# A fused attention and feed-forward block on one core: every fourth clip of the exponentials moves from VectorE to GpSimd

## The chip, the core and the metric

The kernel runs on one core of one Trainium2 chip. The core has five engines that run their own instruction queues and meet only at semaphores: TensorE (matrix products; PE in the profile, its weight loads PEld), VectorE (DVE), ScalarE (ACT), GpSimd (POOL) and SyncE (SP, which here only issues DMAs). The metric is the device time of one execution in microseconds; lower is better.

## The reference, cut to what matters

32 sequences of 100 rows of width 256 attend to a context of 1444 rows each, with 16 heads of width 16, and then go through a quantized feed-forward layer with 704 hidden units:

```
q, k, v = proj(layernorm(x), Wq), proj(ctx, Wk), proj(ctx, Wv)
scores = clip(q @ k.T / 4, -50, 50);  masked positions = -50
probs  = softmax(scores)
x = x + tanh(g0) * layernorm(rs * ((probs @ v) @ Wo.T + bo)) * gamma + beta
h = silu(bitlinear(layernorm(x), w1)) * bitlinear(layernorm(x), w2)
x = x + tanh(g1) * bitlinear(h, w3)
```

The clip of the scores to -50..50 is done after the exponential: the kernel bounds exp(score) from below by exp(-50) and from above by a value per context row, which is exp(50) for a valid row and exp(-50) for a masked one. All in fp32.

## The kernel before

One batch is one of the 32 sequences. Its 1444 context rows are cut into NT = 12 tiles of 121 rows (the last has 113). For every tile TensorE computes the transposed scores of all 16 heads in two halves (line 1327, tile sc), ScalarE exponentiates each half into e_sb (line 619, 121x800 elements), one instruction clips the whole tile in place (line 860, 121x1600), and TensorE multiplies it with v (line 1347, tile pvb). There are six e_sb buffers. The products with v come in blocks of VISIT = 4 tiles, after the scores of slots 1, 5 and 9.

Each engine has a function batch() that loops over twelve slots n = 0 to 11, one for each tile. The order within a slot is written out by hand, and every engine works strictly in that order. Into the slots of batch b the program also puts: the keys and values of batch b+1 (TensorE lines 1368 and 1382; ScalarE k_hi and v_sb; VectorE c_hi, c_lo and k_lo, since fp32 products are made of high and low parts), the layer norm of x of batch b+3 (tiles x_ve, x_rstd, xn), the queries of b+1 (bd, bd_hi, bd_lo, stacked into q_st by twelve DMAs that GpSimd issues), and the output of finished batches: the attention read of pvb, the quotient oT, the product with wo (line 1425), the residual and layer norms, and the feed-forward layer (hq is its quantized hidden row). The 3200 output rows are handled in 25 groups of 128, so 25 of the 32 batches complete a group (full_group).

What GpSimd does in a batch, in this order: in slot 3 it copies the upper bounds of the next batch (mask_of, hi_b) and takes an inverse square root (delta_rstd, d_r), in slot 4 another (x1_rstd), in slot 5 two small factors (ffn_factors), in slot 8 it issues the twelve q_st DMAs (stack_q), and in slot 11 it adds beta to the residual (residual, x_res) and takes the inverse square root for x of batch b+3 (x_rstd_of, x_rstd). VectorE reads that x_rstd in its own slot 11:

```
if nxt2 and b.row + 3 < NB and n == 11:
    x_norm(b.plus(3))          # waits for pool_x, writes xn
...
if n:
    clip(b, n - 1)
```

In VectorE's slot 1 stand the attention read and the inverse of the sums, in slots 1 and 2 the two k_lo of the last third of the context, in slot 2 attention_out (oT) and c_lo of the next batch.

Of the kernel before, what the change touches and what calls it, by code (L numbers as in the profile page):

```python
# [41 lines left out]
def flamingo_block(nc, x, ctxT, maskT, g_xattn, g_ffn, wqT, bq, wkT, bk, wvT, bv, woT, bo,  # L42
# [20 lines left out]
    ALU, ACT, AX = mybir.AluOpType, mybir.ActivationFunctionType, mybir.AxisListType  # L63
# [13 lines left out]
    NT = -(-T // P)  # L77
    TT = -(-T // NT)
    TL = [min(TT, T - n * TT) for n in range(NT)]
# [4 lines left out]
    STEPS = 2  # L84
# [5 lines left out]
    VISIT = 4  # L90
# [10 lines left out]
    E_LO, E_HI = float(np.exp(-CLIP)), float(np.exp(CLIP))  # L101
# [7 lines left out]
    with es:  # L109
# [6 lines left out]
        def sem(name):  # L116
            return es.enter_context(nc.semaphore(name))
# [46 lines left out]
        hi_b = [sb(f"hi_b{i}", [TT, NT]) for i in range(2)]  # L164
# [49 lines left out]
        care_c, care_k, care_v = sem("care_c"), sem("care_k"), sem("care_v")  # L214
        care_x, care_q, care_d, care_y = sem("care_x"), sem("care_q"), sem("care_d"), sem("care_y")
        sc_ready, exp_done = sem("sc_ready"), sem("exp_done")
        clip_done, pv_done = sem("clip_done"), sem("pv_done")
        pe_ctx, pe_x, pe_q, pe_post = sem("pe_ctx"), sem("pe_x"), sem("pe_q"), sem("pe_post")
        split_done, k_lo_done = sem("split_done"), sem("k_lo_done")
        k_hi_done, v_done, act_post = sem("k_hi_done"), sem("v_done"), sem("act_post")  # L220
# [1 line left out]
        act_x, act_q, result_done = sem("act_x"), sem("act_q"), sem("result_done")  # L222
        pool_x, pool_mask, pool_post = sem("pool_x"), sem("pool_mask"), sem("pool_post")

        CLEAN = ("gt", "lt", "pos", "nan", "put_gt", "put_lt")
        SPLIT = Steps(*(f"{p}{u}" for u in range(NCH) for p in ("hi", "lo")))
        CTX = Steps(*(f"{w}{u}{i}" for u in range(NCH) for w in ("k", "v") for i in range(2)))
# [34 lines left out]
        def e_slot(b, n):  # L262
            return (NT * b.par + n) % NE

        def stacked_count(b, u):
            own = b.base or isinstance(b.n, int) and b.n == NB - 1
            return 16 * 3 * NQ * (b.n + 1) - (16 * 3 * (NQ - NQ // 2) if own and u == NCH - 1 else 0)

        def asked(b):

# [169 lines left out]
        def _(pool):  # L440
# [20 lines left out]
            def mask_of(b):  # L461
                pool.wait_ge(s_setv, SETV["hi_all"])
                if b.n >= 2:
                    pool.wait_ge(clip_done, TILE.after(b.plus(-2), NT - 1))
                nc.gpsimd.tensor_copy(hi_b[b.par][:, :],
                                      hi_all[:, :, bass.ds(b.row, 1)].rearrange("p n o -> p (n o)")
                                      ).then_inc(pool_mask, 1)

            def x_rstd_of(b):
                pool.wait_ge(dve_x, X_V.after(b, "var"))  # L470
# [52 lines left out]
            def batch(b, nxt, nxt2=True):  # L523
                gd = full_group(b.plus(-1))
                for n in range(NT):
                    if n == 3:
                        if nxt:
                            mask_of(b.plus(1))
                        if gd:
                            delta_rstd(gd)  # L530
                        if not nxt and not b.base:
                            stack_last(b)
                    if n == 4 and gd:
                        x1_rstd(gd)
                    if n == 5 and gd:
                        ffn_factors(gd)
                    if n == 8 and nxt:
                        stack_q(b.plus(1))
                    if n == 11 and full_group(b):
                        residual(full_group(b))  # L540
                    if n == 11 and nxt2 and b.row + 3 < NB:
                        x_rstd_of(b.plus(3))
# [212 lines left out]
        def _(dve):  # L755
# [97 lines left out]
                                       accum_out=watched(b, KT * u + o)).then_inc(k_lo_done, 1)  # L853

            def clip(b, n):
                dve.wait_ge(exp_done, SCORE.after(b, STEPS * (n + 1) - 1))
                if n == 0:
                    dve.wait_ge(pool_mask, b.n + 1)
                e = e_sb[e_slot(b, n)][0:TL[n], :]
                V.tensor_scalar(e, e, E_LO, hi_b[b.par][0:TL[n], n:n + 1], ALU.max, ALU.min).then_inc(clip_done, 1)  # L860
# [432 lines left out]
        def _(pe):  # L1293
# [37 lines left out]

            def pv(b, n, half, first_batch=False):
                if half == 0:
                    pe.wait_ge(clip_done, TILE.after(b, n))
                    if n % 2 == 0:
                        pe.wait_ge(v_done, VE.after(b, f"{n // TPC}{(n % TPC) // 2}"))
                        if b.base:
                            pe.wait_ge(care_v, GUARD_V.after_row(b, f"{n + 1}1less"))
                    if n == 0 and not first_batch:
                        pe.wait_ge(dve_att, A_V.after(b.plus(-1), "z1"))  # L1340
                e = e_sb[e_slot(b, n)]
                for a in range(2):
                    for j in range(NQ):
                        pr = half * NQ + j
                        col = half * PW + a * S

                        last = T_.matmul(pvb[QR * j:QR * (j + 1), col:col + S],  # L1347
                                         v_sb[0:TL[n], n, pr, a:a + 2, :].rearrange("p x d -> p (x d)"),
                                         e[0:TL[n], pr * PW + a * S:pr * PW + (a + 1) * S],
                                         start=(n == 0 and half == 0 and a == 0), stop=(n == NT - 1),  # L1350
                                         skip_group_check=True)
                if half == 1:
                    last.then_inc(pv_done, 1)
# [267 lines left out]
```

## Time and profile before

| | |
|---|---|
| time, median of 3 runs | 1319.75 us (1317.11 to 1321.18) |
| the profiled execution | 1317.0 us, of which the span of the instructions 1315.2 us |
| TensorE busy | 1292.3 us, 98% of the span |
| VectorE busy | 1080.8 us, 82% |
| ScalarE busy | 951.1 us, 72% |
| GpSimd busy | 361.1 us, 27% |
| clips | 384, 403.0 us of VectorE's time |

The table's busy times are unions over the whole span. An engine that is busy for less than the span had nothing that it was allowed to do in the rest; what it waited for stands in the views of waits and of single instructions.

### The profile page before, as it was taken

Reading aid. Unit: us, or ns where it says so; the run is one execution under the profiler, and the core shown is the slowest. Engines: PE = TensorE matmul, PEld = TensorE weight load, DVE = VectorE, ACT = ScalarE, POOL = GpSimd, SP = SyncE. Lnnn points to the kernel's source line nnn. Section 1 sums busy time; section 2 is a strip of 40 time slices with the busy share of each in tenths; the row PEclk is TensorE's granted clock in tenths of the full one; section 3 lists DMA queues with packets and bytes.
Section 4 is the critical chain, followed back from the end, with each engine's and each line's share of the span. In section 5 each row is a group of like instructions: output and inputs, shape, how many; then the busy total and the mean of one; then the engine's idle time right before and its main releaser. Section 6 shows DMA issues by size and latency. Waiting matters only on the chain.

```text
span 1315.2 us, 47323 instructions
## 1 busy us (share of the span) xinstructions
PE 1292.3 (98%) x19836; PEld 1184.1 (90%) x19836; DVE 1080.8 (82%) x2167; ACT 951.1 (72%) x1576; POOL 361.1 (27%) x594
## 2 busy tenths in 40 slices
PE   8999999999999999999999999999999999999995
PEld 7999999999999989999899999999999999998985
DVE  5789888789888789886889886889778889778875
ACT  3877777867677767776867777777777767777761
POOL 3222223231233231222331222331133331122320
PEclk9999999999999999999999999999999999999989
DMA  7977667766767776777766768776777766767630
GB/s 206 254 175 169 172 164 192 192 168 166 180 155 195 189 170 164 172 166 197 183 170 166 177 159 207 174 170 164 177 186 179 178 170 163 181 174 181 150 87 12
DMA packets 121421, 225.39 MB, mean 171 GB/s; under 512 B 29675, under 2 KB 89871, under 8 KB 121199
## 3 DMA queue, kind: packets, MB, share of 16 engines
q1 hardware_dynamic: 106968, 200.58, 62.3%
q0 software_dynamic: 12576, 20.42, 6.6%
q8 instruction: 159, 2.61, 0.9%
q10 hardware_dynamic: 1654, 1.27, 0.4%
q14 instruction: 64, 0.52, 0.1%
HBM read 57.27 MB, written 3.28 MB: 46 GB/s over the span
## 4 chain that ended last, share of the span: by engine, by line
PE 79%; DVE 13%; issue 3%; POOL 2%; SPq 1%; DMA 1%; ACT 1%; ACTq 1%; DVEq 0%; POOLq 0%
PE sc L1327 19%; PE pvb L1347 18%; PE cb L1382 17%; PE cb L1368 16%; PE mb L1447 2%; DVE e_sb L860 2%; PE mb L1415 2%; DVE c_lo L827 1%; DVE k_lo L851 1%; DVE zt L945 1%; SPq L342 1%; PE mb L1425 1%; PE mb L1462 1%; DMA k_st<-k_lo 1%; PE cb L1531 1%
## 5 line engine op out<-in xcount | busy, mean ns | idle before, releaser
L619 ACT ACTIVATE e_sb<-sc 121x800 f32<-121x800 f32 (+1 forms) x768 | 645.4, 845 | 167.7 <-PE sc L1327 156.1
L1327 PE MATMUL sc<-q_st,k_st 96*121 96x200 f32 (+1 forms) x3072 | 468.1, 275 | 2.9 <-ACT e_sb L619 1.4
L1327 PEld LDWEIGHTS sc<-q_st,k_st 96*121 96x121 f32 (+1 forms) x3072 | 411.1, 185 | 32.3 <-issue 7.8
L860 DVE TENSOR_SCALAR e_sb<-e_sb,hi_b 121x1600 f32<-121x1600 f32 (+1 forms) x384 | 403.0, 1054 | 18.7 <-ACT e_sb L619 18.7
L1347 PEld LDWEIGHTS pvb<-e_sb,v_sb 121*32 121x32 f32 x12288 | 264.5, 110 | 30.6 <-issue 26.4
L1347 PE MATMUL pvb<-e_sb,v_sb 121*32 121x100 f32 x12288 | 286.2, 250 | 1.2 <-DVE e_sb L860 1.2
L851 DVE SCALAR_TENSOR_TENSOR k_lo<-cb,bk_c,k_hi 128x484 fp32r<-128x484 f32 (+1 forms) x192 | 134.6, 701 | 125.5 <-ACT k_hi L631 124.9
L1382 PE MATMUL cb<-wv_hi,c_hi 128*121 128x256 f32 (+1 forms) x768 | 223.1, 290 | 2.4 <-DVE k_lo L851 1.2
L505 POOL DMA_DIRECT2D q_st<-bd_hi x256 | 152.3, 598 | 259.0 <-DVE bd_lo L913 252.9
L1382 PE MATMUL cb<-wv_hi,c_lo 128*121 128x256 f32 (+1 forms) x768 | 216.0, 281 | 0.0
L1382 PE MATMUL cb<-wv_lo,c_hi 128*121 128x256 f32 (+1 forms) x768 | 215.7, 281 | 0.0
L1368 PE MATMUL cb<-c_hi,wk_hi 128*128 128x484 f32 (+1 forms) x384 | 153.2, 399 | 1.4 <-ACT v_sb L640 1.4
L1382 PEld LDWEIGHTS cb<-wv_hi,c_hi 128*121 128x121 f32 (+1 forms) x768 | 141.5, 184 | 6.5 <-DVE k_lo L851 6.3
L1368 PE MATMUL cb<-c_hi,wk_lo 128*128 128x484 f32 (+1 forms) x384 | 145.9, 380 | 0.0
L1368 PE MATMUL cb<-c_lo,wk_hi 128*128 128x484 f32 (+1 forms) x384 | 145.5, 379 | 0.0
L1382 PEld LDWEIGHTS cb<-wv_hi,c_lo 128*121 128x121 f32 (+1 forms) x768 | 140.8, 183 | 0.1
L1382 PEld LDWEIGHTS cb<-wv_lo,c_hi 128*121 128x121 f32 (+1 forms) x768 | 140.2, 183 | 0.0
L631 ACT ACTIVATE k_hi<-cb,bk_c 128x484 fp32r<-128x484 f32 (+1 forms) x192 | 127.0, 661 | 2.0 <-PE cb L1368 1.9
L484 POOL TENSOR_TENSOR d_r<-d_ve,minus_half 128x1 f32<-128x1 f32 x25 | 32.2, 1288 | 344.4 <-DVE d_ve L975 344.4
L827 DVE TENSOR_TENSOR c_lo<-c_in,c_hi 128x968 fp32r<-128x968 f32 (+1 forms) x96 | 117.1, 1220 | 0.0
L640 ACT ACTIVATE v_sb<-cb 121x512 f32<-121x512 f32 x160 | 96.2, 602 | 10.1 <-PE cb L1382 10.1
L1368 PEld LDWEIGHTS cb<-c_hi,wk_lo 128*128 128x128 f32 x384 | 72.1, 188 | 11.7
(165 smaller groups left out, 1358.6 us busy)
## 6 DMA issues: line engine op xcount, KB each, us to landing
k_st<-k_hi SPq DMA_DIRECT2D x508, 121.0 KB, 2.5
c_in<-in_ctxT SPq DMA_DIRECT2D x64, 484.0 KB, 3.9
k_st<-k_lo SPq DMA_DIRECT2D x254, 121.0 KB, 2.5
k_st<-k_hi SPq DMA_DIRECT2D x252, 119.0 KB, 3.2
c_in<-in_ctxT SPq DMA_DIRECT2D x32, 476.0 KB, 3.9
k_st<-k_lo SPq DMA_DIRECT2D x126, 119.0 KB, 3.0
q_st<-bd_hi POOLq DMA_DIRECT2D x256, 50.0 KB, 3.4
q_st<-bd_lo POOLq DMA_DIRECT2D x128, 50.0 KB, 3.5
```

The costliest lines, as they stand in the source:

```text
L484: nc.gpsimd.tensor_tensor(d_r[:, :], d_ve[:, :], minus_half[:, :], ALU.pow).then_inc(pool_post, 1)
L505: nc.gpsimd.dma_start(q_st[b.par][QR * part:QR * (part + 1), j, :, :].bitcast(f32), src[QR * j:QR * (j + 1), :, :, :].rearrange("p k a s - ...
L619: nc.scalar.activation(e_sb[e_slot(b, n)][0:TL[n], k * SW:(k + 1) * SW].rearrange("p (o c) -> p o c", o=2), sc[q % NSC][0:TL[n], :, 0:2 * PW],
L631: nc.scalar.activation(k_hi[slot][:, o, 0:CL[u]], cb[o][:, 0:CL[u]], ACT.Identity, bias=bk_c[:, o:o + 1]).then_inc(k_hi_done, 1)
L640: nc.scalar.activation(v_sb[0:TL[n], n:n + 2, :, 0:3:2, :].rearrange("p n q a d -> p (n q) a d"), cb[i][0:TL[n], :].rearrange("p (q a d) - ...
L827: V.tensor_tensor(c_lo[slot][:, :, 0:w], c_in[slot][:, :, 0:w], c_hi[slot][:, :, 0:w].bitcast(f32), ALU.subtract).then_inc(split_done, 1)
L851: V.scalar_tensor_tensor(k_lo[slot][:, o, 0:w], cb[o][:, 0:w], bk_c[:, o:o + 1], k_hi[slot][:, o, 0:w].bitcast(f32), ALU.add, ALU.subtract ...
L860: V.tensor_scalar(e, e, E_LO, hi_b[b.par][0:TL[n], n:n + 1], ALU.max, ALU.min).then_inc(clip_done, 1)
L1327: last = T_.matmul(sc[q % NSC][0:TL[n], e // 2, (e % 2) * PW:(e % 2 + 1) * PW], k_st[st_slot(b, n // TPC)][:, pr % NQ, pr // NQ, t0:t0 + T ...
L1347: last = T_.matmul(pvb[QR * j:QR * (j + 1), col:col + S], v_sb[0:TL[n], n, pr, a:a + 2, :].rearrange("p x d -> p (x d)"), e[0:TL[n], pr * ...
L1368: last = T_.matmul(cb[o][:, 0:w], wt[:, k, o * P:(o + 1) * P], ct[slot][:, k, 0:w], start=i == 0, stop=i == 5)
L1382: last = T_.matmul(cb[i][0:TL[n], half * H:(half + 1) * H], ct[slot][:, k, t0:t0 + TL[n]], wt[:, k, :], start=(k == 0 and a == 0), stop=(k ...
```

## The change

The clips of tiles 2, 6 and 10 of each batch are issued by GpSimd and signal a semaphore of their own, pool_clip; VectorE clips the other nine. The counts that other engines wait for are adapted, and TensorE waits for pool_clip where the tile is GpSimd's. The instruction is the same (a maximum with a constant, then a minimum with hi_b per partition, in place).

```diff
+        def by_pool(n):
+            return n % VISIT == 2
+
+        def clipped(b, n):
+            return (NT - POOL_CLIPS) * b.n + n + 1 - (n + VISIT - 2) // VISIT
...
+            def clip(b, n):
+                pool.wait_ge(exp_done, SCORE.after(b, STEPS * (n + 1) - 1))
+                e = e_sb[e_slot(b, n)][0:TL[n], :]
+                alone()
+                nc.gpsimd.tensor_scalar(e, e, E_LO, hi_b[b.par][0:TL[n], n:n + 1], ALU.max, ALU.min).then_inc(pool_clip, 1)
...
             def batch(b, nxt, nxt2=True):
                 gd = full_group(b.plus(-1))
                 for n in range(NT):
+                    if n and by_pool(n - 1):
+                        pool.wait_ge(pool_mask, b.n + 1)
+                        clip(b, n - 1)
                     if n == 3:
...
             def clip(b, n):
+                if by_pool(n):
+                    return
                 dve.wait_ge(exp_done, SCORE.after(b, STEPS * (n + 1) - 1))
...
                 if half == 0:
-                    pe.wait_ge(clip_done, TILE.after(b, n))
+                    if by_pool(n):
+                        pe.wait_ge(pool_clip, POOL_CLIPS * b.n + n // VISIT + 1)
+                    else:
+                        pe.wait_ge(clip_done, clipped(b, n))
```

GpSimd's queue around a batch boundary before the change, from the last q_st DMA of one batch (slot 8) over slot 11 to slot 5 of the next:

```order
L505 DMA q_st<-bd_hi 32x400
L478 TENSOR_TENSOR x_res<-x_res,beta_t 128x256
L471 TENSOR_TENSOR x_rstd<-x_ve,minus_half 100x1
L465 COPY hi_b<-hi_all 121x12
L484 TENSOR_TENSOR d_r<-d_ve,minus_half 128x1
L488 TENSOR_TENSOR d_rstd<-d_ve,minus_half 128x1
L493 TENSOR_TENSOR tiny<-tiny,k_tanh 128x1
L496 TENSOR_SCALAR tiny<-tiny,wmean 128x1
L505 DMA q_st<-bd_hi 32x400
```

The same stretch of GpSimd's queue in the changed kernel, whose lines are numbered a little higher:

```order
L520 DMA q_st<-bd_hi 32x400
L482 TENSOR_SCALAR e_sb<-e_sb,hi_b 121x1600
L493 TENSOR_TENSOR x_res<-x_res,beta_t 128x256
L486 TENSOR_TENSOR x_rstd<-x_ve,minus_half 100x1
L482 TENSOR_SCALAR e_sb<-e_sb,hi_b 121x1600
L473 COPY hi_b<-hi_all 121x12
L499 TENSOR_TENSOR d_r<-d_ve,minus_half 128x1
L503 TENSOR_TENSOR d_rstd<-d_ve,minus_half 128x1
L508 TENSOR_TENSOR tiny<-tiny,k_tanh 128x1
L511 TENSOR_SCALAR tiny<-tiny,wmean 128x1
L482 TENSOR_SCALAR e_sb<-e_sb,hi_b 121x1600
L520 DMA q_st<-bd_hi 32x400
```

The clip of tile 10 now stands ahead of x_res and x_rstd, that of tile 2 ahead of hi_b, and that of tile 6 ahead of the DMAs.

VectorE's queue before the change, from slot 10 of a batch to slot 0 of the next (gs, th, tiny and hq belong to the feed-forward layer):

```order
L851 SCALAR_TENSOR_TENSOR k_lo,watch<-cb,bk_c,k_hi 128x484
L1022 SCALAR_TENSOR_TENSOR th<-th,gs 128x352
L860 TENSOR_SCALAR e_sb<-e_sb,hi_b 121x1600
L1028 TENSOR_TENSOR gs<-th,us 128x352
L887 TENSOR_SCALAR xn<-x_in,mv,x_rstd 100x256
L860 TENSOR_SCALAR e_sb<-e_sb,hi_b 121x1600
L1032 TENSOR_REDUCE tiny<-gs 128x1
L860 TENSOR_SCALAR e_sb<-e_sb,hi_b 113x1600
```

The same slots of VectorE's queue in the changed kernel:

```order
L869 SCALAR_TENSOR_TENSOR k_lo,watch<-cb,bk_c,k_hi 128x484
L1042 SCALAR_TENSOR_TENSOR th<-th,gs 128x352
L880 TENSOR_SCALAR e_sb<-e_sb,hi_b 121x1600
L1048 TENSOR_TENSOR gs<-th,us 128x352
L907 TENSOR_SCALAR xn<-x_in,mv,x_rstd 100x256
L1052 TENSOR_REDUCE tiny<-gs 128x1
L880 TENSOR_SCALAR e_sb<-e_sb,hi_b 113x1600
```

The clip of tile 10, between xn and the maximum of the hidden layer, is gone; xn stands where it stood.

## Rows read from the trace of the kernel before

**Rows 1.** Page: the span, and busy time and share of each engine.

```profile
span 1315.2 us, 47323 instructions
...
PE 1292.3 (98%) x19836; PEld 1184.1 (90%) x19836; DVE 1080.8 (82%) x2167; ACT 951.1 (72%) x1576; POOL 361.1 (27%) x594
```

**Rows 2.** Windows: length, busy time of each engine, clock, DMA share, GB/s.

```profile
600.00:1240.00 640.00, 638.40 (x9990) 586.18 (x9992) 538.31 (x1076) 477.60 (x788) 186.01 (x299) 1.00 0.72 175
```

**Rows 3.** Waits between 120 and 1240 us: total us, times, longest.

```profile
DVE k_lo L851 <- ACT k_hi L631: 109.0, 77, 3.9
...
PEld cb L1382 <- DVE k_lo L851: 4.7, 17, 0.4
PEld pvb L1347 <- DVE e_sb L860: 2.0, 6, 0.3
```

**Rows 4.** Groups by form: the full-size clips; busy us, mean ns, idle before.

```profile
L860 DVE TENSOR_SCALAR e_sb<-e_sb,hi_b 121x1600 f32<-121x1600 f32 x352 | 369.6, 1055 | 11.8 <-ACT e_sb L619 11.8
```

**Rows 5.** Groups by form: GpSimd's own instructions.

```profile
L496 POOL TENSOR_SCALAR tiny<-tiny,wmean 128x1 f32<-128x1 f32 x25 | 11.9, 477 | 5.4 <-POOL tiny L493 5.4
...
L493 POOL TENSOR_TENSOR tiny<-tiny,k_tanh 128x1 f32<-128x1 f32 x25 | 4.7, 190 | 78.8 <-DVE tiny L1007 78.8
...
L452 POOL MEMSET v_sb<- 121x1536 f32 x1 | 1.4, 1367 | 0.0
...
L450 POOL TENSOR_SCALAR_AFFINE_SELECT identf<-identf 128x128 f32<-128x128 f32 x1 | 0.3, 284 | 0.3 <-POOL minus_half L447 0.3
...
L447 POOL MEMSET minus_half<- 128x1 f32 x1 | 0.1, 113 | 0.0
```

**Rows 6.** Timeline of GpSimd, 606 to 708 us: start, duration, instruction, idle before.

```profile
608.93 0.50 POOL L505 DMA_DIRECT2D q_st<-bd_lo  x1
...
609.93 0.75 POOL L478 TENSOR_TENSOR x_res<-x_res,beta_t 128x256 f32<-128x256 f32 x1
610.88 0.56 POOL L471 TENSOR_TENSOR x_rstd<-x_ve,minus_half 100x1 f32<-100x1 f32 x1 [0.20 <-DVE x_ve L881]
...
688.47 1.53 POOL L478 TENSOR_TENSOR x_res<-x_res,beta_t 128x256 f32<-128x256 f32 x1
690.34 0.79 POOL L471 TENSOR_TENSOR x_rstd<-x_ve,minus_half 100x1 f32<-100x1 f32 x1 [0.35 <-DVE x_ve L881]
```

**Rows 7.** Timeline of VectorE, 686 to 708 us, slot 11 to slot 2.

```profile
694.07 0.41 DVE L887 TENSOR_SCALAR xn<-x_in,mv,x_rstd 100x256 f32<-100x256 f32 x1
694.39 1.04 DVE L860 TENSOR_SCALAR e_sb<-e_sb,hi_b 121x1600 f32<-121x1600 f32 x1
...
701.43 0.42 DVE L934 TENSOR_SCALAR pT<-pvb,submask 128x200 f32<-128x200 f32 x1 [0.51 <-PE pvb L1347]
...
704.77 0.61 DVE L851 SCALAR_TENSOR_TENSOR k_lo<-cb,bk_c,k_hi 128x476 fp32r<-128x476 f32 x1
...
705.31 0.36 DVE L951 TENSOR_TENSOR oT<-pT,zt 128x200 f32<-128x200 f32 x1
...
706.94 1.16 DVE L827 TENSOR_TENSOR c_lo<-c_in,c_hi 128x968 fp32r<-128x968 f32 x1
```

**Rows 8.** Timeline of ScalarE: second halves of tile 10 and tile 2.

```profile
692.58 0.88 ACT L619 ACTIVATE e_sb<-sc 121x800 f32<-121x800 f32 x1
...
705.18 0.84 ACT L619 ACTIVATE e_sb<-sc 121x800 f32<-121x800 f32 x1 [0.53 <-PE sc L1327]
```

**Rows 9.** Timeline of TensorE, 705 to 710 us.

```profile
706.12 0.29 PE L1382 MATMUL cb<-wv_hi,c_hi 128*121 128x256 f32 x1
...
706.84 1.03 PE L1425 MATMUL mb<-wo,oT 128*128 128x256 f32 x4
...
709.24 0.40 PE L1368 MATMUL cb<-c_hi,wk_hi 128*128 128x484 f32 x1
```

**Rows 10.** Timelines of VectorE around 608 and 688 us: c_lo.

```profile
608.28 1.67 DVE L827 TENSOR_TENSOR c_lo<-c_in,c_hi 128x952 fp32r<-128x952 f32 x1
...
688.27 1.14 DVE L827 TENSOR_TENSOR c_lo<-c_in,c_hi 128x952 fp32r<-128x952 f32 x1
```

More of the change, by code:

```diff
@@ L216, in flamingo_block @@
         sc_ready, exp_done = sem("sc_ready"), sem("exp_done")
-        clip_done, pv_done = sem("clip_done"), sem("pv_done")
+        clip_done, pool_clip, pv_done = sem("clip_done"), sem("pool_clip"), sem("pv_done")
         pe_ctx, pe_x, pe_q, pe_post = sem("pe_ctx"), sem("pe_x"), sem("pe_q"), sem("pe_post")
@@ L223, in flamingo_block @@
         pool_x, pool_mask, pool_post = sem("pool_x"), sem("pool_mask"), sem("pool_post")
+        POOL_CLIPS = 3
         CLEAN = ("gt", "lt", "pos", "nan", "put_gt", "put_lt")
@@ L463, in mask_of @@
                 if b.n >= 2:
-                    pool.wait_ge(clip_done, TILE.after(b.plus(-2), NT - 1))
+                    pool.wait_ge(clip_done, clipped(b.plus(-2), NT - 1))
                 nc.gpsimd.tensor_copy(hi_b[b.par][:, :],
```

## The prediction

> **What bounds the kernel now.** I read the header and the busy line of the page first, then the engines' busy time in a long stretch, then the waits, and last the timelines of one batch boundary. The span is 1315.2 us, and TensorE is busy for 1292.3 us of it [rows 1]. Between 600 and 1240 us it is busy for 638.4 of 640 us at a granted clock of 1.00 [rows 2]: in the steady part of the kernel TensorE never stands still. What it waits for there is tiny: between 120 and 1240 us its weight loads waited 4.7 us for k_lo and 2.0 us for clipped tiles [rows 3]. VectorE is busy for 82% of the span [rows 1] and has holes, above all while it waits for ScalarE's k_hi, 109.0 us in the same stretch [rows 3]. So VectorE is not the bound, but it feeds the bound. A faster VectorE can give back at most what TensorE waits for, and every microsecond by which something TensorE needs comes too late is a microsecond of the kernel's time.
>
> **What is taken away.** Three of twelve clips in each of 32 batches leave VectorE: 96 instructions of 1.055 us [rows 4], 101 us of its 1080.8. Since TensorE waited some 7 us for VectorE in the steady part, this is worth 0 to 7 us by itself. I take 0: the gain is used up as soon as one of the waits below appears.
>
> **What is added: the length of a GpSimd clip.** No 1600-column computation of GpSimd is in this trace, so I bound its duration D from other rows [rows 5]. A two-operation TENSOR_SCALAR with an operand per partition takes 0.477 us on one column: that is the fixed part. The slope is between two rows. A memset writes 1536 columns in 1.367 us and one column in 0.113, 0.82 ns a column: D = 0.48 + 1.31 = 1.8 us. An addition with two inputs takes 0.75 us on 256 columns at its fastest [rows 6] against 0.19 us for a product on one column [rows 5], 2.2 ns a column: D = 0.48 + 3.5 = 4.0 us. The nearest row is the affine select, one input read and something computed on each element: 0.284 us for 128 columns, less 0.113, is 1.33 ns a column: D = 2.6 us. I take 2.4, a little below, since a part of the select's time is a fixed one that the memset doesn't have. Either way the clip is about twice as long as on VectorE.
>
> The Trainium skill (GPSIMD Engine Reference, section 4.1) calls one-input work on GpSimd roughly line-rate. By that the columns would take 1.3 us at the 1.2 GHz which the same page states, an estimate that lies below my lower bound, and the sum below would shrink to a few microseconds.
>
> **First wait: the queue behind the clip of tile 10.** TensorE needs tiles 2, 6 and 10 only in its PV blocks, more than 5 us after they are exponentiated, so the clips themselves are in time. What stands behind them in GpSimd's queue is not. In slot 11 GpSimd used to run the residual and x_rstd as soon as the q_st DMAs were issued: x_rstd ended at 690.34 + 0.79 = 691.1 [rows 6], and VectorE read it in xn at 694.07 [rows 7]. Now both stand behind the clip of tile 10, which waits for ScalarE's exponential, finished at 692.58 + 0.88 = 693.46 [rows 8]. Add D, 0.75 for the residual and 0.56 for x_rstd [rows 6]: xn can start at 694.8 + D, that is D + 0.7 late. If VectorE's own work must first let GpSimd in (next part), up to 0.7 more. Behind xn on VectorE's queue stand the clip of tile 11, the hidden layer's quantization, the last two k_lo, the attention read and oT. The lag shrinks by the clip of tile 10 that is gone (1.04 at 694.39) and by the 0.51 that VectorE used to stand idle before the attention read at 701.43 [rows 7]. What is left at the k_lo of 704.77 is D - 0.8 to D - 0.1. That k_lo ended at 704.77 + 0.61 = 705.38 [rows 7], and TensorE used it at 706.12 [rows 9]: slack 0.74. So TensorE stands still for D - 1.5 to D - 0.8, with D = 2.4 for 0.9 to 1.6 us.
>
> **Second wait: two engines at one SBUF port.** The trace shows that VectorE and GpSimd hold each other up. The same c_lo subtraction takes 1.14 us at 688.27 and 1.67 us at 608.28 [rows 10], and in the second case GpSimd's DMA issue of 0.50 us begins at 608.93 [rows 6], while c_lo is under way. The other way round, the residual takes 0.75 us alone and 1.53 us when it starts at 688.47 [rows 6], 0.2 us into the c_lo of 688.27: it ends only after c_lo has. So whoever is second waits until the first is done. The Trainium skill (SBUF — State Buffer, section "Who interferes with whom") says just this of fp32 tensor_scalar and of instructions with two SBUF inputs on VectorE against any GpSimd instruction that reads; the trace agrees. By that rule a clip on GpSimd takes a stretch of D away from VectorE's clips, c_lo and oT where before a clip of 1.05 us stood, and in the sum it is the difference between the two values that follow.
>
> The exponential of tile 2 ends at 705.18 + 0.84 = 706.02 [rows 8], and the idle GpSimd starts at once. VectorE's oT, which had started at 705.31 [rows 7], is by then late by the lag above, so it finds the port taken, ends at 706.02 + D + 0.36, and TensorE's product with wo, due at 706.84 [rows 9], starts D - 0.4 late. That is counted from TensorE's old times, so it contains the first wait instead of adding to it: 2.0 us for D = 2.4. The c_lo behind it (706.94 to 708.10, needed at 709.24 [rows 7, 9]) is then no later than TensorE itself.
>
> **The sum.** Both steps need a batch with a full row group (residual and wo product now) after one with a hidden layer under way. Of the 29 boundaries with an xn three batches ahead, 25 groups in 32 batches leave 15 such. 15 x 2.0 = 30 us. In the other 14 the residual or the hidden layer's work is missing and the first wait is mostly absorbed, but the clip of tile 2 still meets clip 1 and c_lo: from nothing to D less c_lo's slack of 1.14, 1.3 us; I take the middle, 0.65, so 9 us. Setup and tail: 0. Together 39 us. The profiled execution had 1317.0 us of time around a span of 1315.2, so it would read 1356; against the median of 1319.75, **1359 us**, +3.0%.
>
> Other moves cost nothing. The clip of tile 6 delays the twelve q_st DMAs behind it by up to D, but GpSimd then waits for tile 10's exponential anyway, and TensorE asks for q_st only in the next batch; the residual used to start at 688.47 behind the last of them [rows 6], 5 us before that exponential [rows 8]. Were this cover gone, TensorE would wait up to D for q_st in each batch. delta_rstd, behind the clip of tile 2, is wanted by VectorE only after the wo product, which waits longer. SP's queue is untouched.
>
> **The rivals.**
> - A slower clip: D from 3 to 4 us. Then 15 x 3.6 and 14 x 2.9 at the upper end, +95: 1375 to 1415. For it speaks that residual and rstd on this engine are slow for their size.
> - Small loss: D = 1.8, GpSimd gets in at once, oT isn't blocked. 15 x 0.3 = 5 us, up to 15 with something from the rest: 1324 to 1335. The line-rate rule of the Trainium skill (GPSIMD Engine Reference, section 4.1) would lead here or below.
> - No change, 1320: D below 1.5 and no block. Only the slack of 0.74 at k_lo and that of the wo product have to hold [rows 7, 9].
> - Faster: VectorE's 101 us of relief are what TensorE's 7 us of waits come from, and nothing new is late. It takes D under 1.3, so that xn is on time within the clip saved, and gives 1312 to 1315. Against it: the memset row alone puts D at 1.8.
>
> **How the numbers follow.** Two measurements of this kernel can be told apart from about 0.3%, 4 us. Forecast (1335 to 1375): 0.60. Slower clip: 0.15. Small loss: 0.12. No change: 0.08. Faster: 0.05. Slower altogether 0.87. The range that leaves no more than 0.2 out is 1326 to 1400; it takes in most of both neighbours of the forecast.
>
> **What the changed profile would show.** GpSimd's clip at 2.4 us (1.8 to 4.0) x96. VectorE's clips x288. A wait of xn for x_rstd, 2 to 4 us in most batches, some 80 us in all, where now it is nothing. TensorE waiting for k_lo and oT, 1 to 2 us a time, its busy share in the steady part down from 99.8% to about 97%; c_lo or oT with durations above 2 us where they meet a GpSimd clip. The prediction is wrong if xn doesn't wait, if D is under 1.5, or if VectorE's late work is absorbed before TensorE asks for it; then the time stays near 1320. If TensorE waits for the GpSimd clips themselves, or for q_st, it is worse than I say.

## The result and the profile after

The changed kernel takes **1656.22 us** (median of 4 runs, 1650.04 to 1665.12) against 1318.43 us for the kernel before in the same comparison (4 runs, 1315.49 to 1321.18): ratio 1.2565, 95% interval 1.2527 to 1.2603. That is 338 us slower. The forecast was 1359 us: the direction was right, the size far off, and the time lies outside the range.

The header and busy line of the page of the changed kernel, which answer to [rows 1]:

```profile
span 1663.3 us, 47418 instructions
...
PE 1421.0 (85%) x19836; PEld 1279.9 (77%) x19836; DVE 1245.5 (75%) x2071; ACT 966.0 (58%) x1576; POOL 942.3 (57%) x690
```

The span grew by 348.1 us (the profiled run was the slowest of the four, 1665.12 us). TensorE stands still for 1663.3 - 1421.0 = 242.3 us instead of 22.9, so 219 us are new waits. The other 129 us are busy time: the same 19836 products take 1421.0 us instead of 1292.3. VectorE has 96 instructions less and is busy for 165 us more.

Two windows of the changed kernel (length, busy time of PE, PEld, DVE, ACT and POOL, granted clock, DMA share, GB/s), the first of which answers to [rows 2]:

```profile
600.00:1240.00 640.00, 552.12 (x7800) 497.45 (x7801) 477.64 (x805) 382.07 (x623) 372.97 (x270) 0.92 0.56 139
850.00:860.00 10.00, 8.20 (x36) 7.40 (x37) 8.72 (x17) 3.98 (x8) 5.56 (x4) 0.66 0.44 119
```

The granted clock of the steady part fell from 1.00 to 0.92; in the ten microseconds behind a long wait it averages 0.66, so TensorE ran there for a good part at 1.2 GHz instead of 2.4.

The groups of instructions of the changed kernel. The number behind the second bar is the idle time of the engine just before them, and what ended it:

```profile
L482 POOL TENSOR_SCALAR e_sb<-e_sb,hi_b 121x1600 f32<-121x1600 f32 x96 | 568.2, 5919 | 479.6 <-issue 473.9
...
L880 DVE TENSOR_SCALAR e_sb<-e_sb,hi_b 121x1600 f32<-121x1600 f32 (+1 forms) x288 | 490.5, 1703 | 53.2 <-ACT e_sb L637 53.1
...
L907 DVE TENSOR_SCALAR xn<-x_in,mv,x_rstd 100x256 f32<-100x256 f32 x32 | 18.6, 581 | 193.8 <-POOL x_rstd L486 193.8
```

A clip on GpSimd takes 5.92 us on average, 5.65 at its shortest, where I had put 2.4. VectorE's 288 clips take 1703 ns on average instead of some 1055 [rows 4]. xn waits 193.8 us for x_rstd; before it never did.

TensorE's waits in the changed kernel (total us, times, longest):

```profile
PE cb L1391 <- DVE c_lo L845: 56.3, 13, 5.3
PE sc L1347 <- issue: 47.6, 29, 5.0
PE mb L1448 <- DVE y_out L1074: 36.8, 13, 3.4
PE pvb L1370 <- DVE e_sb L880: 24.2, 21, 2.0
PE cb L1405 <- DVE k_lo L869: 23.6, 21, 1.8
PE mb L1448 <- DVE oT L971: 15.5, 5, 3.3
```

With 12.0 us for hq they make 216 us, nearly all of the 219. The second row is TensorE's first scores of a batch, which wait for q_st (the runs below show it).

One batch boundary shows the mechanism. GpSimd, 846 to 890 us in the changed kernel (start, duration, instruction, idle before), answering to [rows 6]:

```profile
846.78 5.65 POOL L482 TENSOR_SCALAR e_sb<-e_sb,hi_b 121x1600 f32<-121x1600 f32 x1 [8.63 <-issue]
...
868.55 6.07 POOL L482 TENSOR_SCALAR e_sb<-e_sb,hi_b 121x1600 f32<-121x1600 f32 x1 [3.73 <-issue]
874.58 0.99 POOL L520 DMA_DIRECT2D q_st<-bd_hi  x1
...
881.09 0.50 POOL L520 DMA_DIRECT2D q_st<-bd_hi  x1
882.16 6.19 POOL L482 TENSOR_SCALAR e_sb<-e_sb,hi_b 121x1600 f32<-121x1600 f32 x1 [0.58 <-issue]
888.33 0.73 POOL L493 TENSOR_TENSOR x_res<-x_res,beta_t 128x256 f32<-128x256 f32 x1
889.03 0.56 POOL L486 TENSOR_TENSOR x_rstd<-x_ve,minus_half 100x1 f32<-100x1 f32 x1
```

VectorE in the same stretch of the same kernel, answering to [rows 7]:

```profile
847.88 3.38 DVE L971 TENSOR_TENSOR oT<-pT,zt 128x72 f32<-128x72 f32 x2
851.18 0.47 DVE L1074 SCALAR_TENSOR_TENSOR y_out<-mb,tiny,x 128x256 f32<-128x256 f32 x1
851.58 1.70 DVE L880 TENSOR_SCALAR e_sb<-e_sb,hi_b 121x1600 f32<-121x1600 f32 x1
...
870.82 4.65 DVE L880 TENSOR_SCALAR e_sb<-e_sb,hi_b 121x1600 f32<-121x1600 f32 x1 [1.64 <-ACT e_sb L637]
...
889.62 0.42 DVE L907 TENSOR_SCALAR xn<-x_in,mv,x_rstd 100x256 f32<-100x256 f32 x1 [6.72 <-POOL x_rstd L486]
```

And TensorE, answering to [rows 9]:

```profile
851.80 2.05 PE L1448 MATMUL mb<-wo,oT 128*128 128x256 f32 x4 [2.82 <-DVE y_out L1074]
...
856.50 0.66 PE L1391 MATMUL cb<-c_hi,wk_hi 128*128 128x484 f32 x1
...
884.92 0.64 PE L1347 MATMUL sc<-q_st,k_st 96*121 96x200 f32 x4 [1.18 <-issue]
```

Read in order: GpSimd begins the clip of tile 2 at 846.78. oT (here two instructions in one row) starts 1.1 us later and takes 3.38 us instead of 0.36; it ends at 851.26, which is 1.17 us before GpSimd's clip does. The clip behind it ends at 853.28, 0.85 us after GpSimd's clip (852.43). The clip that VectorE starts at 870.82, while GpSimd clips tile 6, takes 4.65 us and ends at 875.47, again 0.85 us after GpSimd's 874.62. After the clip of tile 10 comes xn, for which VectorE stood idle for 6.72 us. TensorE waits 2.82 us for the product with wo, and then the product takes 2.05 us instead of the 1.03 of [rows 9]: half the clock, right behind the wait. The q_st DMAs end at 881.6, and TensorE waits for them at 884.92.

### The profile page after: what moved, and what is told of

The parts are those of the page before. It is cut to its first block and busy times, and to the rows that moved or that the text cites. A ratio compares the mean times of both kernels' runs of the same rounds, so it can differ in the third digit from the quotient of the medians.

```text
span 1663.3 us, 47418 instructions
## 1 busy us (share of the span) xinstructions
PE 1421.0 (85%) x19836; PEld 1279.9 (77%) x19836; DVE 1245.5 (75%) x2071; ACT 966.0 (58%) x1576; POOL 942.3 (57%) x690
## 5 line engine op out<-in xcount | busy, mean ns | idle before, releaser
L482 POOL TENSOR_SCALAR e_sb<-e_sb,hi_b 121x1600 f32<-121x1600 f32 x96 | 568.2, 5919 | 479.6 <-issue 473.9
L1347 PE MATMUL sc<-q_st,k_st 96*121 96x200 f32 (+1 forms) x3072 | 509.7, 292 | 48.9 <-issue 47.6
L880 DVE TENSOR_SCALAR e_sb<-e_sb,hi_b 121x1600 f32<-121x1600 f32 (+1 forms) x288 | 490.5, 1703 | 53.2 <-ACT e_sb L637 53.1
L1347 PEld LDWEIGHTS sc<-q_st,k_st 96*121 96x121 f32 (+1 forms) x3072 | 451.3, 201 | 88.8 <-issue 60.6
L1391 PE MATMUL cb<-c_hi,wk_hi 128*128 128x484 f32 (+1 forms) x384 | 173.7, 452 | 58.9 <-DVE c_lo L845 56.3
L907 DVE TENSOR_SCALAR xn<-x_in,mv,x_rstd 100x256 f32<-100x256 f32 x32 | 18.6, 581 | 193.8 <-POOL x_rstd L486 193.8
L1391 PE MATMUL cb<-c_lo,wk_hi 128*128 128x484 f32 (+1 forms) x384 | 160.9, 419 | 0.0
L1391 PE MATMUL cb<-c_hi,wk_lo 128*128 128x484 f32 (+1 forms) x384 | 159.7, 416 | 0.0
L1391 PEld LDWEIGHTS cb<-c_hi,wk_hi 128*128 128x128 f32 x384 | 84.2, 219 | 61.5 <-DVE c_lo L845 58.5
L845 DVE TENSOR_TENSOR c_lo<-c_in,c_hi 128x968 fp32r<-128x968 f32 (+1 forms) x96 | 110.4, 1150 | 0.0
```

Of the source, the lines that this page charges most:

```text
L482: nc.gpsimd.tensor_scalar(e, e, E_LO, hi_b[b.par][0:TL[n], n:n + 1], ALU.max, ALU.min).then_inc(pool_clip, 1)
L845: V.tensor_tensor(c_lo[slot][:, :, 0:w], c_in[slot][:, :, 0:w], c_hi[slot][:, :, 0:w].bitcast(f32), ALU.subtract).then_inc(split_done, 1)
L907: norm = V.tensor_scalar(xn[:, :], x_in[b.par][:, :], mv[:, 0:1], x_rstd[:, :], ALU.subtract, ALU.mult)
L1347: last = T_.matmul(sc[q % NSC][0:TL[n], e // 2, (e % 2) * PW:(e % 2 + 1) * PW], k_st[st_slot(b, n // TPC)][:, pr % NQ, pr // NQ, t0:t0 + T ...
L1391: last = T_.matmul(cb[o][:, 0:w], wt[:, k, o * P:(o + 1) * P], ct[slot][:, k, 0:w], start=i == 0, stop=i == 5)
```

## The experiments

Twelve kernels ran. Each was compared with the kernel before on the same chip (1320.1 us for forms, part560, order11 and queue0; 1319.88 for tile2, tile6, tile10 and mult; 1319.12 for queue5, tile10_order, filled and pieces).

### forms: what the operation costs on a GpSimd that does nothing else

The kernel before, with seven instructions of GpSimd on a scratch tile behind all its work:

```diff
+            form(G.tensor_scalar, t, t, E_LO, hi, ALU.max, ALU.min)
+            form(G.tensor_scalar, t[:, 0:400], t[:, 0:400], E_LO, hi, ALU.max, ALU.min)
+            form(G.tensor_scalar, t, t, E_LO, E_HI, ALU.max, ALU.min)
+            form(G.tensor_scalar, t, t, E_LO, None, ALU.max)
+            form(G.tensor_scalar, t, t, hi, None, ALU.min)
+            form(G.tensor_scalar, t, t, 1.0, 0.0, ALU.mult, ALU.add)
+            form(G.tensor_copy, t[:, 0:400], t[:, 400:800])
```

> The kernel before, with seven instructions added behind GpSimd's last one, on a private tile of 121 partitions, each waiting for the one before. It measures the disputed duration by itself, nearly without VectorE beside it. Theory A, the clip costs a fixed 0.5 us and 3.4 to 3.5 ns a column whatever VectorE does: the same clip on 800 columns takes 3.2 us and on 400 columns 1.9 us. Theory B, most of the 5.9 us is waiting for VectorE's instructions: 800 columns take about 1.4 us, as a memset's 0.82 ns a column would give. If the cost is one per operation, a single maximum or minimum on 800 columns takes about half of the double one; if it is a cost of reading and writing an element, single and double ones take the same.

The timeline of GpSimd at the end of that kernel, one row for each instruction in the order of the diff:

```profile
1301.42 2.96 POOL L571 TENSOR_SCALAR tst<-tst,hi_b 121x800 f32<-121x800 f32 x1
1304.58 1.61 POOL L571 TENSOR_SCALAR tst<-tst,hi_b 121x400 f32<-121x400 f32 x1 [0.20 <-POOL tst L571]
1306.39 2.98 POOL L571 TENSOR_SCALAR tst<-tst 121x800 f32<-121x800 f32 x1 [0.20 <-POOL tst L571]
1309.56 2.22 POOL L571 TENSOR_SCALAR tst<-tst 121x800 f32<-121x800 f32 x1 [0.19 <-POOL tst L571]
1311.99 2.28 POOL L571 TENSOR_SCALAR tst<-tst,hi_b 121x800 f32<-121x800 f32 x1 [0.22 <-POOL tst L571]
1314.46 0.86 POOL L571 TENSOR_SCALAR tst<-tst 121x800 f32<-121x800 f32 x1 [0.19 <-POOL tst L571]
1315.49 0.51 POOL L571 COPY tst<-tst 121x400 f32<-121x400 f32 x1 [0.17 <-POOL tst L571]
```

800 columns in 2.96 us and 400 in 1.61 make (2.96 - 1.61) / 400 = 3.4 ns a column and 0.26 us fixed, so 1600 columns take 5.66: just the shortest clip of the changed kernel, 5.65. The operand per partition is innocent (2.98 with a constant). The cost is in the maximum and the minimum: one of them takes 2.2 us for 800 columns, a product and a sum together 0.86. VectorE ran some short instructions beside the first four and none beside the last three; one maximum (2.22) and one minimum (2.28) take the same with and without them. So GpSimd by itself is that slow.

### part560: a clip as short as the one I had assumed

The whole change, but GpSimd clips 560 columns of its tiles and VectorE the other 1040:

```diff
-                nc.gpsimd.tensor_scalar(e, e, E_LO, hi_b[b.par][0:TL[n], n:n + 1], ALU.max, ALU.min).then_inc(pool_clip, 1)
+                nc.gpsimd.tensor_scalar(e[:, 0:560], e[:, 0:560], E_LO, hi_b[b.par][0:TL[n], n:n + 1], ALU.max, ALU.min).then_inc(pool_clip, 1)
...
-                e = e_sb[e_slot(b, n)][0:TL[n], :]
+                e = e_sb[e_slot(b, n)][0:TL[n], 560 if by_pool(n) else 0:EW]
```

> The changed kernel, but GpSimd clips only columns 0 to 559 of tiles 2, 6 and 10 and VectorE columns 560 to 1599, so that GpSimd's clip takes about the 2.4 us that the forecast assumed (0.5 + 560 x 3.45 ns = 2.4). Theory A, only the duration was wrong and the sum was right for its own D: 39 us over before, 1357 us. Theory B, the cost goes in proportion to D (338 us for 5.9 us): 137 us over before, 1455 us. Theory C, the slacks were underrated and the loss begins only with a longer clip: below 1330 us.

1364.84 us, ratio 1.0339 (1.0314 to 1.0364), +45 us. GpSimd's clip:

```profile
L482 POOL TENSOR_SCALAR e_sb<-e_sb,hi_b 121x560 f32<-121x560 f32 x96 | 241.3, 2514 | 517.6 <-issue 491.4 <-ACT e_sb L637 26.2
```

With D = 2.51 my sum gives 15 x 2.11 + 14 x 0.69 = 41 us; 45 were measured. xn waits 93 us in all (I had said some 80), and the clock stays at 0.995. Near the length that I assumed, the total holds, in part by luck. Of the 47.5 us by which the span is longer, 36 are waits of TensorE and 12 are busy time. The waits are for k_lo (27.8 us), hq (7.8) and c_lo (3.7). There is none for oT or y_out, on which 15 x 2.11 rests. One boundary of this kernel, GpSimd's clip, oT and TensorE's product behind k_lo:

```profile
731.85 2.16 POOL L482 TENSOR_SCALAR e_sb<-e_sb,hi_b 121x560 f32<-121x560 f32 x1 [9.30 <-issue]
732.95 0.36 DVE L969 TENSOR_TENSOR oT<-pT,zt 128x200 f32<-128x200 f32 x1
733.09 0.38 PE L1403 MATMUL cb<-wv_hi,c_hi 128*121 128x256 f32 x1 [1.19 <-DVE k_lo L869]
```

oT runs beside the clip at its old length. The first wait of the prediction is there, as large as it said (1.19 us, within D - 1.5 to D - 0.8), and the second is not.

### order11: the queue's wait taken away

The whole change, with the residual and x_rstd ahead of the clip of tile 10:

```diff
-                    if n and by_pool(n - 1):
+                    if n and by_pool(n - 1) and n < 11:
...
                         x_rstd_of(b.plus(3))
+                    if n == 11 and by_pool(n - 1):
+                        pool.wait_ge(pool_mask, b.n + 1)
+                        clip(b, n - 1)
```

> The changed kernel with one thing moved: in slot 11 GpSimd runs the residual and x_rstd ahead of the clip of tile 10 instead of behind it. All three clips stay on GpSimd at their full length. Theory A, most of the loss is the queue behind the clip of tile 10 (xn waited 193.8 us): those waits vanish and the time falls by 150 to 200 us, to 1450 to 1500 us. Theory B, most of it is the port, VectorE held for the length of each GpSimd clip, and the wait of xn only hides what would show elsewhere: the time falls by less than 60 us, to above 1595 us.

1647.15 us, ratio 1.2473 (1.244 to 1.2506): 9 us of the 338 come back. xn's wait for x_rstd fell from 193.8 to 16.7 us, but nothing was won. GpSimd's three instructions in one slot 11 of this kernel:

```profile
864.82 0.86 POOL L493 TENSOR_TENSOR x_res<-x_res,beta_t 128x256 f32<-128x256 f32 x1
865.65 0.56 POOL L486 TENSOR_TENSOR x_rstd<-x_ve,minus_half 100x1 f32<-100x1 f32 x1
866.22 5.67 POOL L482 TENSOR_SCALAR e_sb<-e_sb,hi_b 121x1600 f32<-121x1600 f32 x1
```

And VectorE in the same slot:

```profile
865.01 7.73 DVE L883 TENSOR_SCALAR e_sb<-e_sb,hi_b 121x1600 f32<-121x1600 f32 x1
873.09 0.40 DVE L910 TENSOR_SCALAR xn<-x_in,mv,x_rstd 100x256 f32<-100x256 f32 x1
```

x_rstd is ready at 866.21, and VectorE still comes to xn only at 873.09: its own clip stands at the port for 7.73 us. It had started at 865.01, before x_rstd (865.65) and before GpSimd's clip (866.22), and both went ahead of it. In other batches xn itself stands there, whose mean rose from 581 to 2756 ns. The port takes the place of the queue in VectorE's order; the waits of TensorE stay (for y_out 47.2 us, k_lo 32.9, c_lo 32.8, q_st 48.1).

### queue0 and queue5: the queue's wait alone, with no clip on GpSimd

Both are the kernel before with one more wait of GpSimd in slot 11, ahead of the residual and x_rstd; all clips stay on VectorE. queue0 waits for the exponential of tile 10 and gives the wait without D:

```diff
+                    if n == 11:
+                        pool.wait_ge(exp_done, SCORE.after(b, STEPS * n - 1))
                     if n == 11 and full_group(b):
```

> The kernel before, all clips on VectorE, with one wait added: GpSimd's residual and x_rstd of slot 11 wait for the exponential of tile 10, as they do in the changed kernel, but no clip stands between. xn is then about 0.7 us late. By the forecast's slacks (0.51 idle and 0.74 at k_lo, with no clip taken from VectorE) this is just absorbed: 1318 us, within 0.3%. If it costs more than 5 us, the slacks at this place were overrated.

1325.42 us, ratio 1.0043 (1.0022 to 1.0064): 5.3 us, just over the 5 that I had set: the wait alone, with a clip of no length at that place, would already cost a little. queue5 waits for the next batch's first exponentials instead, about as long as the clip lasts:

```diff
+                    if n == 11 and nxt:
+                        pool.wait_ge(exp_done, SCORE.after(b.plus(1), 1))
```

> The kernel before with all twelve clips on VectorE and no clip on GpSimd, but the residual and x_rstd of slot 11 wait for the first tile's exponential of the next batch, which comes about 4 us after that of tile 10. xn is then 4.8 us late, with no port held. Theory A, the queue wait costs by itself what the slacks say: 4.8 less 0.51 and 0.74, 3.6 us in 15 boundaries and some of it in the others, 1375 to 1400 us. Theory B, without the port VectorE catches up: below 1335 us.

1423.92 us, ratio 1.0795 (1.077 to 1.082), +105 us. xn waits 149.4 us; TensorE's waits are many and short (k_lo 37.0 us in 39, the longest 1.2; e_sb 32.2 us in 45, the longest 1.2), and the clock stays at 0.993. The queue alone does such damage without a clip at the port. It is more than either end of what I had expected: my lag left TensorE's PV blocks out, where tile 11's clip, behind xn, is asked for early (19.8 of the 32.2 us are in front of the products of tile 11).

### tile2, tile6 and tile10: one clip on GpSimd at a time

```diff
-            return n % VISIT == 2
+            return n in POOL_TILES
```

POOL_TILES holds 2, 6 or 10 alone, and the counts of the semaphores follow.

> GpSimd clips tile 2 alone, VectorE the other eleven. x_rstd is not behind a clip, so the queue wait is out. Theory A, the port: GpSimd starts at the exponential of tile 2, VectorE's clip 1, c_lo or oT is held for up to 5.7 us, and c_lo has 1.14 us of slack: about 4.6 us in most of 31 batches, 1430 to 1530 us with what the clock adds. Theory B, the queue is what counts: within 1% of before.

> GpSimd clips tile 6 alone. In the changed kernel TensorE stood idle for 47.7 us in front of the first scores of a batch, which need q_st, and the q_st DMAs stand behind the clip of tile 6. Theory A, that wait is this clip's: some 1 to 2 us in most batches, 1335 to 1375 us, with the wait at the same place. Theory B, the wait comes from the whole schedule being late: within 1% of before.

> GpSimd clips tile 10 alone, with the residual and x_rstd behind it. By the forecast's sum for D = 5.9 the first wait is D + 0.7 less 1.04, 0.51 and 0.74, so 4.3 us in 15 boundaries and less in the others: 65 to 110 us over before, 1385 to 1430 us, plus what the clock adds, with waits of xn of about 6.5 us. If the three single runs add up to the 338 us of the whole change, the losses are independent; if they add up to clearly more, one hides behind the other.

| clip on GpSimd | us | ratio (95%) | more than before | clock | TensorE waits most for |
|---|---|---|---|---|---|
| tile 2 | 1437.29 | 1.0901 (1.0853 to 1.0948) | 117 | 0.963 | k_lo 36.5, c_lo 18.1, oT 13.3 |
| tile 6 | 1415.42 | 1.0712 (1.0675 to 1.075) | 96 | 0.970 | q_st 61.1 |
| tile 10 | 1452.04 | 1.0997 (1.0955 to 1.1039) | 132 | 0.965 | e_sb 56.8, k_lo 15.8, hq 11.9 |

117 + 96 + 132 = 345, against 338 for all three: each clip has its own wait, and they add. So do the parts: TensorE stands still for 74, 64 and 85 us more than before, together 223 (219 in the changed kernel), and is busy for 43, 40 and 51 us more, together 134 (129). tile2 is in the range of its theory A; tile10 is 22 us above its range, which left the clock out, with waits of xn of 6.5 us as expected. The clip of tile 6, which the prediction put at nothing and my expectation for this run at less than was measured, costs 96 us. Its rows for TensorE's scores and VectorE's clips in tile6:

```profile
L1348 PE MATMUL sc<-q_st,k_st 96*121 96x200 f32 (+1 forms) x3072 | 483.0, 281 | 63.4 <-issue 61.1 <-ACT e_sb L638 1.4 <-DMA k_st<-k_lo 0.7
...
L881 DVE TENSOR_SCALAR e_sb<-e_sb,hi_b 121x1600 f32<-121x1600 f32 x320 | 451.7, 1414 | 31.0 <-ACT e_sb L638 31.0
```

The first scores of a batch wait 30 times, 2.0 us a time; in tile10, where that clip is VectorE's, the same group has 2.9 us of idle time in all and none of it at issue. So it is the q_st DMAs behind the clip of tile 6. In tile2 the port works the other way round as well. GpSimd:

```profile
730.30 7.40 POOL L483 TENSOR_SCALAR e_sb<-e_sb,hi_b 121x1600 f32<-121x1600 f32 x1 [15.10 <-issue]
```

VectorE at the same time:

```profile
730.13 1.04 DVE L881 TENSOR_SCALAR e_sb<-e_sb,hi_b 121x1600 f32<-121x1600 f32 x1
731.09 1.16 DVE L846 TENSOR_TENSOR c_lo<-c_in,c_hi 128x968 fp32r<-128x968 f32 x1
```

VectorE's clip and its c_lo run at their old durations until 732.25, and GpSimd's clip ends at 737.70, which is 5.45 us after that: it got hardly any work done until both were through, although c_lo was started 0.79 us after it. Its mean in that kernel is 6.9 us.

### mult: the same places, a quicker operation

GpSimd multiplies by 1 and adds 0; the clip of tiles 2, 6 and 10 is left out of the computation.

```diff
-                nc.gpsimd.tensor_scalar(e, e, E_LO, hi_b[b.par][0:TL[n], n:n + 1], ALU.max, ALU.min).then_inc(pool_clip, 1)
+                nc.gpsimd.tensor_scalar(e, e, 1.0, 0.0, ALU.mult, ALU.add).then_inc(pool_clip, 1)
```

> The changed kernel with GpSimd's instruction on tiles 2, 6 and 10 replaced by a product with 1 and a sum with 0, so the clip of these tiles is left out. The form took 0.86 us on 800 columns where the clip took 2.96, so about 1.6 us on 1600: the duration that the rival with the small loss assumed. Theory A, the sum follows D: 5 to 20 us over before, 1324 to 1340 us. Theory B, a second user at the port costs by itself, whatever its duration: above 1360 us.

1358.69 us, ratio 1.0288 (1.0253 to 1.0323), +39 us, with an instruction of 1.74 us on average and a clock of 0.994. That is more than the 1340 that I had allowed. My sum with D = 1.74 gives 15 x 1.34 + 14 x 0.3 = 24 us, and the rival called small loss gave 5 to 15: both are too low at the short end. TensorE stands still for 31 us more than before and is busy for 10 us more, which is no term of the sum. Here the product with wo does wait for y_out and oT (17.6 us), and the boundaries without one wait for c_lo (8.4). Still, one and the same change with 1.7 us in place of 5.9 costs 39 us in place of 338.

### tile10_order: tile10 with x_rstd ahead of the clip

The edit of order11 on top of tile10.

> GpSimd clips tile 10 alone, as in the single run, but behind the residual and x_rstd instead of ahead of them, so that xn no longer waits in GpSimd's queue. Theory A, port and queue stand in for each other: xn itself, the clip of tile 9 or the product before it then finds the port held, its duration grows to several microseconds and the time stays within 2% of the 1452 us of the single run. Theory B, for this tile the queue is the loss: below 1350 us.

1410.09 us, ratio 1.0703 (1.0682 to 1.0725), 42 us less than tile10. Neither theory had that: with the queue's wait gone, about two thirds of the loss (91 of 132 us) are still there, now behind the port. xn itself now takes 3923 ns on average (413 in tile10), and the clip of tile 11 behind it 2144 (1397). TensorE's waits are short again (the longest for k_lo 1.2 us, for VectorE's e_sb 1.4, against 2.6 in tile10), and the clock is back at 0.992 from 0.965; busy time fell from 1343.2 to 1313.7 us. Of the 44 us of span, 30 are busy time that came back with the clock, and 15 are waits.

### filled: products without use in two of TensorE's waits

The whole change, plus 18 and 27 small products into the free bank pvb, ahead of the product with wo and of the first key product of a batch without one. The profile shows each as two instructions:

```diff
+            def filler(b, count):
+                pe.wait_ge(dve_att, A_V.after(b, "z1"))
+                for _ in range(count):
+                    T_.matmul(pvb[:, 0:P], ones[:, :], ones[:, :], start=True, stop=True)
```

> The changed kernel with products of a constant tile added on TensorE where it waited longest: 18 ahead of the product with wo, and 27 ahead of the first k product in slot 4 of batches that have no product with wo. The results aren't used. At full clock they last 2.4 and 3.6 us, about as long as the waits of 2.8 and 4.3 us there. Theory A, a part of the loss is that the granted clock falls after such waits (0.66 in the ten microseconds from 850 on, and TensorE is busy for 129 us longer than before with the same work): with the waits filled the clock stays near 1 and the time falls by 30 to 100 us, to 1555 to 1625 us. Theory B, the lower clock costs nothing, since TensorE waits for VectorE anyway: 1650 us or more.

1624.32 us, ratio 1.231 (1.2276 to 1.2345): 32 us faster than without, with 1242 more instructions. These take 143.8 us of busy time, 4.2 and 6.2 us in a row where I had estimated 2.4 and 3.6, so they outlast the waits that they fill. What is left of TensorE's 1490.6, the real work, takes 1346.8 us instead of 1421.0, at a mean clock of 0.964 instead of 0.916. So 74 us of the 129 us of new busy time came back once these two waits were filled, and the clock with them. No other instruction was changed, so the clock is a cause of its own.

### pieces: the clip cut in four

The whole change, with four instructions of 400 columns where there was one of 1600:

```diff
+                for i in range(4):
+                    c = slice(400 * i, 400 * (i + 1))
+                    piece = nc.gpsimd.tensor_scalar(e[:, c], e[:, c], E_LO, hi_b[b.par][0:TL[n], n:n + 1], ALU.max, ALU.min)
+                piece.then_inc(pool_clip, 1)
```

> The changed kernel with each GpSimd clip cut into four instructions of 400 columns, one behind the other, 1.61 us each by the forms, 6.4 us in all instead of 5.7. Theory A, the port is held for one instruction and VectorE gets in between two: no VectorE instruction is held for more than 1.6 us, and the time falls, to 1450 to 1600 us, although GpSimd works longer. Theory B, what counts is when GpSimd's clip ends, or VectorE gets in no earlier: 1650 us or more.

1588.2 us, ratio 1.2008 (1.1946 to 1.2071): 68 us faster than in one piece. GpSimd's pieces and VectorE's clips:

```profile
L484 POOL TENSOR_SCALAR e_sb<-e_sb,hi_b 121x400 f32<-121x400 f32 x384 | 752.9, 1972 | 360.8 <-issue 360.2
...
L883 DVE TENSOR_SCALAR e_sb<-e_sb,hi_b 121x1600 f32<-121x1600 f32 x256 | 283.2, 1106 | 38.2 <-ACT e_sb L640 38.2
```

VectorE's clips are back at 1106 ns (the longest takes 1.41 us), and now GpSimd pays: 1972 ns for a piece that takes 1615 alone, 7.9 us a tile. With shorter instructions the other engine gets in between. xn waits even longer (222.3 us), and TensorE now waits 45.1 us for GpSimd's tiles themselves.

## Why the prediction failed, step by step

**The step that failed is "What is added: the length of a GpSimd clip".** I bounded D by 1.8 and 4.0 us and took 2.4; it is 5.92 on average, and 5.66 by the two lengths in forms. The fixed part, 0.48 for 0.26, did no harm. The slopes came from a memset, an affine select and an addition, 0.82 to 2.2 ns a column [rows 5, 6], and none of these rows has a maximum or a minimum in it; the clip has both, at 3.4 ns a column. A product and a sum in the same instruction form do run within these slopes, at 1.1 ns a column (0.86 us for 800, 1.74 for 1600). Taking the bounds as the ends of what is possible was the error: they bound other operations. The Trainium skill (GPSIMD Engine Reference, section 4.1) calls one-input work roughly line-rate; the product with a sum agrees (0.86 us for 800 columns), the clip doesn't. This step is not the whole miss: with the right D my sum reaches some 1435 to 1470 us (below). The rest is mostly q_st and the clock, which I had put at nothing.

**The two waits were right in kind, the port's rule only in part.** xn starts D + 0.7 late by the text, and VectorE waits 6.72 us for it in the batch shown. VectorE's clips are held to the end of GpSimd's clip, as the text said. oT is not: it ends 1.17 us before that in the batch shown, and in part560 it is hardly held at all (0.81 us at most), so "ends at 706.02 + D + 0.36" was wrong. Of the two rows from which I read the port, the residual's 1.53 us shows it. The c_lo of 1.67 us does not: it was first, the DMA issue behind it kept its 0.50 us, and another c_lo of the kernel before, with an issue at the same place, takes 1.13:

```profile
569.85 1.13 DVE L827 TENSOR_TENSOR c_lo<-c_in,c_hi 128x952 fp32r<-128x952 f32 x1
...
570.51 0.50 POOL L505 DMA_DIRECT2D q_st<-bd_hi  x1
```

What lengthened the first one stays open. The Trainium skill (SBUF — State Buffer, section "Who interferes with whom") describes the lock as held for a whole instruction, by whichever engine issued first. For the whole instruction VectorE's clips agree (4.65 us beside a clip, 1.41 at most in pieces). For the order the traces do not always agree: in order11 VectorE's clip and in tile2 GpSimd's was overtaken by instructions that started later, when the other engine had several in a row. With the queue wait removed (order11) the port's wait stands in its place, as the text's "contains the first wait instead of adding to it" implies, though in tile10 alone two thirds of the loss remained.

**The sum was fair for the waits that it had, and it lacked others.** With D = 5.92 it gives 15 x 5.5 = 83 us, and for the other 14 boundaries, by the middle and the upper end of my rule, 33 to 67: together 116 to 150 us, so about 1435 to 1470 us, not 1656. The measured parts, from TensorE's single waits (sorted by the boundary that they fall in) and the span, each less what it was before:

| part | forecast with D = 5.92 | measured |
|---|---|---|
| the 15 boundaries with residual and hidden layer | 83 | 87 |
| the other 14 | 33 to 67 | 70 |
| q_st, behind the clip of tile 6 | 0 | 46 |
| setup, the last batches and the tail | 0 | 17 |
| busy time of TensorE, mostly the clock | 0 | 129 |

That the first row fits is in part luck: by the sum it is all in front of the product with wo. Measured are 30 us there, 19 in PV blocks, 18 for c_lo, 13 for k_lo and 7 for hq. The product with wo waits more for y_out (36.8 us) than for oT (15.5): it writes into the bank mb, which y_out still reads, and y_out stands behind oT.

**"Other moves cost nothing" failed for q_st.** I named the cover and the price of losing it, and dismissed it, without measuring the cover against a D beyond my bounds. The kernel before, GpSimd's last q_st DMA and the scores that need it:

```profile
687.44 1.01 POOL L505 DMA_DIRECT2D q_st<-bd_hi  x1
...
695.07 0.57 PE L1327 MATMUL sc<-q_st,k_st 96*121 96x200 f32 x4
```

695.07 - 688.45 = 6.6 us, less 2.9 to 3.4 for the landing (medians of the pages of the changed kernel and of the one before) leaves 3.2 to 3.7. A clip of 2.4 hides there, and part560 has no such wait; one of 5.9 misses by 2.2 to 2.7, and 47.6 us in 29 waits is 1.6 a time.

**The clock is missing from the prediction altogether.** The mean granted clock of the whole span is 0.994 before and 0.916 after. The 1292.3 us at the one make some 1402 at the other, an estimate, so about 110 of the 129 us are the clock. The rest also appears where the clock is whole: queue5 has 1317.4 us of busy time at 0.993, 25 more than before, after many short stops. The sum of the waits doesn't tell what the clock does: queue5 loses 105 us in many waits of about 1 us and keeps its clock, while tile6 loses 96 us in 30 waits of 2 us on average and up to 4.2, and has 0.970; the changed kernel, with single waits up to 5.3 us, has 0.916. The Trainium skill (TensorE: Matmul & The Clock Gate, section "HAM oscillation — how this bites in real kernels") describes a kernel in which the clock falls during each wait for data, so that the products behind it start slow; 2.05 us for the wo product here against 1.03 [rows 9] agrees. This and q_st make the loss steeper than the lag: D of 1.74, 2.51 and 5.92 us give +39, +45 and +338 us.

**The range and the rivals.** "Slower clip" was the right rival, but its D ended at 4. What would have shown the error is in the text: "If TensorE waits ... for q_st, it is worse than I say".

**Open.** mult costs 39 us and not 24: its trace has 10 us more of busy time, and 11 us more of waits than before in the other 14 boundaries, where the sum has 4. Why was not tried. The 48 us of q_st were not tested by DMAs ahead of the clip in the whole change, and that 110 of the 129 us are the clock is an estimate from a mean. No version that ran beats the kernel before.

## What to carry to other kernels

Before work moves to GpSimd, time that very operation on that engine: a bound from its other instructions says nothing when the arithmetic differs, and the maximum and minimum took over five times as long there as on VectorE (5.65 us against 1.05). Then count what stands behind it in GpSimd's queue, and take a VectorE instruction of the kind of the clips that meets it as held to its end. A kernel whose TensorE never stands still can lose more than its waits: here the product behind one of 2.82 us ran at half the clock.

## What was not expected of the hardware

- GpSimd, 121 x 800 fp32 in place: maximum and minimum 2.96 us, one of them 2.22 to 2.28, product and sum 0.86.
- A VectorE clip that is held does nearly all of its work behind GpSimd's: in all 66 cases in the changed kernel it ends 0.84 to 0.85 us after GpSimd's clip, and by itself it takes 1.05. oT, with two inputs, ends 1.2 to 1.4 us before the GpSimd clip that holds it (23 cases), but 0.2 us after GpSimd's product and sum in mult (median of 25). Why they differ was not tested.
- VectorE back to back can hold GpSimd as well: 7.40 us for a clip of 5.65 in tile2. The other way round, three GpSimd instructions in a row held a VectorE clip for 7.73 us in order11.
- Products without use in TensorE's waits made a kernel 32 us faster.
